# Attention masks after the exponential: three score tiles of a unit on GpSimd instead of two

## The reference, cut to what matters

```
scores = einsum('bhqd,bhkd->bhqk', q, k) / sqrt(D_HEAD)
scores = where(mask == 0, -1e9, scores)      # one 512 x 512 mask for all
attn   = softmax(scores, axis=-1)
out    = einsum('bhqk,bhkd->bhqd', attn, v)
```

## Time and profile before

| | us |
|---|---|
| median of 3 runs | 2750.9 (2750.63 to 2751.59) |
| the profiled execution | 2753.34 |
| its span in the trace | 2751.6 |
| TensorE busy | 2629.1 |
| VectorE busy | 2192.3 |
| ScalarE busy | 1742.5 |
| GpSimd busy | 1719.2 |
| masks on GpSimd (L2024), 112 of them | 162.7 |

### The profile page before, as it was taken

One profiled execution on the slowest core, in us unless ns is written; L12 is line 12 of the kernel. 1 busy time (PEld: TensorE's weight loads), 2 busy tenths in 40 slices (PEclk: granted clock), 3 DMA queues, 4 the chain that ended last, 5 costly groups with the idle time before them and its releaser, 6 DMA issues. The chain is left out here.

```text
span 2751.6 us, 55526 instructions
## 1 busy us (share of the span) xinstructions
PE 2629.1 (96%) x19177; PEld 1799.8 (65%) x19210; DVE 2192.3 (80%) x3270; ACT 1742.5 (63%) x2871; POOL 1719.2 (62%) x966
## 2 busy tenths in 40 slices
PE   6999999999999999999999879999999999999996
PEld 3887787787878877877887754545454545454523
DVE  5999999999999999999998949494848485858573
ACT  4878877877987788788778433545454444444342
POOL 3889989988988889899899813332323232323130
PEclk9999999999999999999999999999999999999978
DMA  3122212212221221222123051404040404040300
GB/s 123 43 79 73 85 44 81 89 43 79 74 80 43 80 82 58 70 67 95 37 78 102 9 182 55 123 2 122 2 122 2 122 2 122 2 122 2 107 2 16
DMA packets 102089, 187.07 MB, mean 68 GB/s; under 512 B 14720, under 2 KB 75264, under 8 KB 100256
## 3 DMA queue, kind: packets, MB, share of 16 engines
q1 hardware_dynamic: 101840, 183.92, 21.4%
HBM read 148.38 MB, written 35.52 MB: 67 GB/s over the span
## 5 line engine op out<-in xcount | busy, mean ns | idle before, releaser
L981 DVE TENSOR_TENSOR_SCAN h<-dA,pair 128x512 f32<-128x512 f32 x1024 | 1171.2, 1202 | 113.6 <-PE pair L475 102.9
L1120 POOL TENSOR_TENSOR hC<-h,C_rep 128x1024 f32<-128x1024 f32 x512 | 1201.4, 2368 | 93.5 <-DVE h L981 87.3
L718 ACT ACTIVATE dA<-delta,cols 128x511 f32<-128x511 f32 x1024 | 664.2, 711 | 41.7 <-DVE h L981 25.6
L475 PE MATMUL pair<-diagB,duT 64*128 64x128 f32 x8192 | 549.3, 281 | 23.1 <-DVE h L981 14.1
L475 PEld LDWEIGHTS pair<-diagB,duT 64*128 64x128 f32 x8192 | 485.9, 188 | 125.7 <-issue 90.1
L575 PE MATMUL y_bank<-ident,hC 128*128 128x128 f32 x4112 | 539.4, 278 | 5.0 <-POOL hC L1120 4.1
L575 PEld LDWEIGHTS y_bank<-ident,hC 128*128 128x128 f32 x4112 | 458.3, 141 | 96.9 <-issue 55.1
L1897 DVE CUSTOM_DVE_ANT_0 masked<-pair,mask_bias 128x512 f32<-128x512 f32 x512 | 321.8, 688 | 19.4 <-PE pair L1376 13.5
L1629 ACT ACTIVATE pr<-pair 128x1024 f32<-128x1024 f32 x256 | 248.3, 1021 | 74.3 <-PE pair L1376 74.3
L2001 POOL CAST m_part<-m_rest 8x512 bf16<-8x512 f32 x16 | 9.6, 603 | 414.4 <-ACT m_rest L1629 414.4
L475 PE MATMUL general<-xnT,w_in 128*128 128x512 f32 x496 | 241.9, 602 | 4.5 <-ACT xnT L718 3.5
(11 more groups left out here) (185 smaller groups left out, 3197.1 us busy)
## 6 DMA issues: line engine op xcount, KB each, us to landing
C_rep<-c_rows SPq DMA_DIRECT2D x128, 512.0 KB, 4.2
qk_parts<-qk_part SPq DMA_DIRECT2D x96, 256.0 KB, 4.2
w_in<-w_in SPq DMA_DIRECT2D x16, 1024.0 KB, 4.9
k_st<-qk_parts SPq DMA_DIRECT2D x8, 1536.0 KB, 9.1
q_st<-qk_parts SPq DMA_DIRECT2D x8, 1536.0 KB, 9.4
x_in<-x SPq DMA_DIRECT2D x18, 512.0 KB, 5.3
w_out<-w_out SPq DMA_DIRECT2D x17, 512.0 KB, 4.2
mid<-x_out SPq DMA_DIRECT2D x9, 512.0 KB, 4.8
```

Source lines behind the costliest of these rows:

```text
L475: return pe.matmul(o, lhsT, rhs, start=start, stop=stop)
L718: return act.activation(o, i, fn, **kw)
L981: last = dve.tensor_tensor_scan(h[:, g % 4, i, :], dA[:, g % 4, i, :], dBu[:, i, :], 0.0, ALU.mult, ALU.add)
L1120: pool.tensor_tensor(hC[:, g % RING], h[:, g % 4], C_rep[:, 2 * j:2 * j + 2, :], ALU.mult).then_inc(s_hC.sem, 1)
```

## The change

`ON_POOL` goes from one head in each half to two heads in the first and one in the second. `score` leaves out one more bias product in each unit from 1 to 7, that of head 0; `mask_exp` for half 0 covers heads 0 and 1 in one operation of 128x1024 (it was 128x512), and still waits for the exponential of head 1 (`heads[-1]`). Nothing else differs: the number of masks, the semaphore counts and the order of every engine stay.

```diff
@@ -41,7 +41,7 @@
-ON_POOL = ((1,), (3,))
+ON_POOL = ((0, 1), (3,))
```

## The result

The changed kernel takes 2757.85 us (median of 9 runs, 2752.55 to 2760.38) against 2750.9 before (9 runs, 2749.11 to 2754.11). The ratio is 1.0024, with a 95% interval of 1.0015 to 1.0033: some 7 us slower (4 to 9). The forecast was 2757.5 us, 6.6 more than before. The profiled execution took 2755.85 us, its span is 2754.1. One execution of e1 (4000.94 us) and one of e5 (6311.89 us) were slow ones, and medians and ratios leave them out, as they do the slow ones of the kernel before.

The account below looks back on a forecast made before the run. TensorE was taken to bound the steady loop, with GpSimd and VectorE excluding each other next. Seven elements 1.0 us longer, less 0.35 in the eighth, gave +6.6 us on 2750.9: 2757.5 us, range 2744 to 2768.

Parts of the forecast that it names:

- Six products of 0.22 us in an element: TensorE, unit loop: seven bias products go, unit 1's gains nothing, six save 1.3 us an element if nothing becomes late.
- A two-head mask is 2.36 us: GpSimd, half 0: the 128x1024 mask takes 2.36 us, as an f32 tensor-tensor of that size; ends 2.2 and 2.54.
- the third rival: GpSimd: the two-head mask costs twice a single, 2.54 us; +16 us, 2767; chance 0.12.
- GpSimd and VectorE exclude each other and take turns: Unit loop: each waits for the other's operation, then they alternate; VectorE's contended operations in steps 2 to 4 take 3.2 us.
- 35.2 us from the first mask to the last's end: Unit loop: GpSimd's 25.4 us and VectorE's 13.3, less 3.5 for handovers, make 35.2 us of exclusive time.
- The last weigh 1.0 us later: Loop's end: last mask late, TensorE idle 2.6 us, the weigh and so the element 1.0 us later, in seven elements.
- The placing one behind the other: Unit loop: masks and VectorE operations lined up by the turn rule; the last mask ends at 2012.1.
- Cover of the store and of `normalise(2)`: Loop's end: later `finish` and store, and `normalise(2)` at 2011.1, cost nothing, with 1 us to spare.
- The eighth element's last weigh 0.35 us earlier: Last element, VectorE idle 11.17 us: -1.3 without the wait and 1.0 of wait added make the last weigh 0.35 us earlier.
- The fourth rival: TensorE's clock falls in the new 2.6 us wait, costing 4 us in each of seven elements; +35, 2786; chance 0.03.

Follow-up runs that it names:

- e1: Changed kernel, but TensorE keeps head 0's bias product as in the kernel before, so that tile is masked twice; 2759.78 us, ratio 1.0032 to the kernel before.
- e5: Kernel before, with the two-head mask and the missing bias product only in units 2 to 5; 2747.76 us, ratio 0.9987.
- e2: Kernel before, with head 0's bias product left out but GpSimd's masks unchanged, so one tile stays unmasked; 2741.38 us, ratio 0.9963.
- e4: Changed kernel with VectorE's spiking steps 1 to 4 left out; 2731.9 us, ratio 0.9928 to the kernel before.
- e7: The changed kernel again, nothing altered, timed beside other runs; 2757.88 us, ratio 1.0024 to the kernel before.
- e3: Kernel before, with VectorE's spiking steps 1 to 4 left out; 2740.56 us, ratio 0.9965.
- e6: Changed kernel with heads 0 and 1 masked by two operations of 128x512 in place of one of 128x1024; 2762.29 us, ratio 1.0042 to the kernel before.
- e9: Changed kernel with the next element's first key projection moved ahead of the unit loop's last weigh; 2753.06 us, ratio 1.0001 to the kernel before.

## Why the prediction was right, point by point

- *Six products of 0.22 us in an element.* e2: 1.32 us in the period, so one of the seven is worth nothing, as forecast for unit 1's.
- *A two-head mask is 2.36 us.* It takes 2.36 alone, so the third rival, with 2.54, is out.
- *GpSimd and VectorE exclude each other and take turns.* Operations of 3.23 us were forecast at 3.2; e4 shows the cause. The Trainium skill's rule (SBUF — State Buffer, Who interferes with whom) holds: the loser waits for the whole instruction, 3.23 us for 1.23 behind a mask of 2.36. That the other engine is next is what the traces add.
- *35.2 us from the first mask to the last's end.* It is 35.1.
- *The last weigh 1.0 us later.* It comes 0.78 us later, behind a wait of 2.35 us for 2.6. The placing one behind the other put the mask 0.2 us too late.
- *Cover of the store and of `normalise(2)`.* `finish` ends 34.0 us behind the first mask (34.2 forecast), 3.8 us later than before. ScalarE's first evacuation of `project_k` starts at 2013.59, 3.0 us behind the last weigh as before.
- *The eighth element's last weigh 0.35 us earlier.* It is 36.23 us behind the first mask against 36.70: 0.47.
- *The fourth rival, 0.03, as an alternative.* Here the forecast was wrong in kind: the clock's fall is no other case but an addition to the forecast one, in two elements of seven and at 1.5 us each, not 4. With it the sum is 7 x 0.78 - 0.47 + 2 x 1.5 = 8.0. From the first mask to the end the profile has 7.0: the stretch behind the eighth element's last weigh is 1.3 us shorter than before, and the seventh period has 0.3 more than the 0.78. In e7's trace, with the same kernel, it is 8.6, for there that last stretch is 0.3 us longer than before. That the forecast of 6.6 came so near to the measured 7 is in part luck: two errors, 1.5 us too much for the weighs and 3.0 too little for the clock, pull against each other, and the last stretch, which the sum put at nothing, varies by as much.
- *The profiled span.* It grew by 2.5 us only, since the first mask comes at 1701.15 in it and at 1705.69 before. Nothing of the change stands ahead of it, and in the nine traces of the experiments it lies between 1699.4 and 1704.4. Why the first pass varies was not looked into.

Left open: why e3, with less work, has a period 0.4 us longer than the kernel before. TensorE's matmuls follow each other as before until 64.6 us behind the last weigh; there, in the next element's prescore, they fall 0.3 us behind.

## What to carry to other kernels

Work moved to GpSimd was paid for in VectorE's time as well. Where the two engines' operations exclude each other, as here, add both between the first and the last deadline, and compare that sum, not GpSimd's busy share, with the bounding engine's time. Where it fits only in part, move work in the stretches with gaps and leave the last units alone; the same four masks gave 0.87 us an element early and nothing late. And a wait on the bounding engine may cost more than its length: two of seven cost 1.5 us each on top.

## What the runs showed that was not expected

TensorE's granted clock fell to 0.50 for some 3 us at an idle time of 2.3 us in four of 14 such waits, and at 1.80 us in three of seven (e6, whose TensorE had further waits of about 0.5 us in the same loop). From the seventh element's last weigh to the eighth's first mask it was at 0.50 for 34 to 44 us in every kernel, so seventh periods compare less well than the first six. In the last element it fell earlier in the traces of e2, e5 and e9 than in the others, and the output projection there took 2.4 to 2.8 us longer; where whole executions are compared, that hides a third of a gain of 7 us.
